# Layers 0 and 1 of a four-layer convolution net: the spectrum, the statistics and the group average spread over the slots of an image

## The reference

```python
# _gn: mean and variance of each pair of channels over an image; (x - mean) / sqrt(var + 1e-5)

def layer0(x, W, b):                       # x is _gn(x)
    offsets = jnp.mean(x, axis=(1, 2)) @ W + b
    dy, dx = jnp.clip(offsets, 0, 28).astype(jnp.int32)   # one pair for an image
    return the image moved down by dy rows and right by dx columns, zeros where nothing comes

def layer1(x, W, b):                       # 3 x 3 convolution of signs
    xq = jnp.where(x >= 0, 1.0, -1.0)
    w_sum = jnp.where(W >= 0, 1.0, -1.0).sum(axis=0)
    return conv(xq, w_sum, padding="SAME") + b.sum(axis=0)

x = x + layer0(_gn(x)); x = x + layer1(_gn(x))
```

## Time and profile before

| what | value |
|---|---|
| median of 3 runs | 4056.27 us (4055.71 to 4059.10) |
| the profiled execution | 4058.18 us |
| its span, first to last instruction | 4056.4 us |
| mean granted TensorE clock | 0.852 of full |
| layers 0 and 1 (last instruction on an `A_` tile) | until 2203 us |

### The profile page before, as it was taken

The page is one execution under the profiler, slowest core; times in us unless marked ns, Lnnn a source line. Parts: engine busy times, 40 slices in busy tenths (PEclk is TensorE's granted clock), DMA queues, the critical chain, the costliest instruction groups (busy, mean ns, idle before and its releaser), DMA issues. The chain is left out here.

```text
span 4056.4 us, 58465 instructions
## 1 busy us (share of the span) xinstructions
PE 3117.6 (77%) x17264; PEld 1421.0 (35%) x17264; DVE 2755.7 (68%) x3864; ACT 1483.0 (37%) x2708; POOL 36.9 (1%) x23
## 2 busy tenths in 40 slices
PE   0277877787877877778786579988998964799997
PEld 0133333333333333233333533333333324344443
DVE  3777665766577656766651557777677744599998
ACT  3455653655455544565433422222222214000000
POOL 0000000000000000000000000000000001000000
PEclk9987886888788877788887589999999976799998
DMA  4666544654466445655433475655665516799998
GB/s 144 176 183 199 160 155 130 203 169 150 131 188 203 141 130 163 203 160 155 139 111 107 93 293 213 251 214 205 240 247 201 219 61 125 270 379 387 390 385 305
DMA packets 272195, 808.65 MB, mean 199 GB/s; under 512 B 85466, under 2 KB 119774, under 8 KB 261108
## 3 DMA queue, kind: packets, MB, share of 16 engines
q1 hardware_dynamic: 212948, 488.15, 37.9%
q10 hardware_dynamic: 58368, 316.72, 20.3%
q0 software_dynamic: 608, 0.63, 0.1%
HBM read 479.39 MB, written 329.56 MB: 199 GB/s over the span
## 5 line engine op out<-in xcount | busy, mean ns | idle before, releaser
L817 DVE SCALAR_TENSOR_TENSOR A_image<-A_cps,A_cbias,A_image 128x896 f32<-128x896 f32 x224 | 257.3, 1149 | 492.0 <-PE A_cps L455 491.7
L1371 ACT ACTIVATE B_junk<-B_im,B_nk 128x896 bf16<-128x896 f32 x224 | 232.8, 1039 | 724.9 <-DVE B_im L1429 585.1
L455 PE MATMUL A_cps<-A_sign,A_cfull 128*128 128x448 bf16 x1344 | 448.9, 421 | 11.3 <-issue 11.3
L595 ACT ACTIVATE A_tout<-A_aps 112x512 f32<-112x512 f32 x448 | 244.5, 589 | 531.9 <-PE A_aps L482 531.5
L482 PE MATMUL A_aps<-a_k_ident,A_image 128*112 128x128 f32 x1792 | 313.5, 331 | 140.5 <-DVE A_image L817 124.5
L1622 PE MATMUL C_ring<-C_im,C_wnorm 128*128 128x448 f32 x896 | 388.9, 573 | 23.0 <-DVE C_ubuf L1679 17.8
L460 PE MATMUL A_cps<-A_sign,A_cedge 32*32 32x448 bf16 x1344 | 405.3, 415 | 0.0
L462 PE MATMUL A_cps<-A_sign,A_cedge 32*32 32x448 bf16 x1344 | 404.9, 414 | 0.0
L1317 PE MATMUL B_ring<-B_im,B_wnorm 128*128 128x448 f32 x896 | 384.5, 570 | 7.7 <-DVE B_wnorm L1400 5.5
L496 PE MATMUL A_vps<-A_tout,a_k_dctj 112*32 112x512 f32 x896 | 289.3, 780 | 118.3 <-ACT A_tout L595 118.2
L1289 PE MATMUL B_ring<-B_rout,iB_k_rowf 128*64 128x512 f32 x896 | 282.2, 714 | 118.3 <-DVE B_rout L1422 118.3
(11 more groups left out here) (193 smaller groups left out, 3436.5 us busy)
## 6 DMA issues: line engine op xcount, KB each, us to landing
A_rin<-in_x SPq DMA_DIRECT2D x2016, 112.0 KB, 2.4
x2s<-A_image ACTq DMA_DIRECT2D x112, 896.0 KB, 4.6
B_im<-x2s SPq DMA_DIRECT2D x112, 896.0 KB, 9.7
x3s<-B_im ACTq DMA_DIRECT2D x112, 896.0 KB
C_im<-x3s SPq DMA_DIRECT2D x112, 896.0 KB, 11.9
out<-C_rout ACTq DMA_DIRECT2D x192, 256.0 KB
out<-C_rout ACTq DMA_DIRECT2D x192, 192.0 KB
out<-C_rout ACTq DMA_DIRECT2D x64, 128.0 KB
```

The lines of the kernel that those rows point to most:

```text
L455: return nc.tensor.matmul(banks[:, s, 0:LPN], cfull[:, tap, :], lines(n, s, slice(0, P), 0, tap), start=(tap == 0), stop=(tap == 2), skip_ ...
```

## The change

- The two tables of tiles start at once and are even: 3 tiles in most slots from slot 0 on. X tiles come first within a slot, in slot 0 ahead of unit 0's add.
- The spectrum's 8 items go two to a slot in slots 0 to 3, one before and one after `forward_cols` and `turn_back`; the rows of an item follow in the next step, the last ones in slot 4. Results go to a bank `wps` of their own, shared with the statistics (`mps` is now its first 16 columns), and to a store buffer `specout` of their own. The copy moves to slot 5 and the store from slot 4 to slot 6.
- The statistics of the next image begin in slots 11 and 12 in place of 13 and 14. Part 2 is cut in two (2 and 4); the second, behind the root, comes after the signs. ACT takes the root in slot 13, and `lower` is in slot 14 ahead of the square.
- The group average is on PE after unit 13's convolution. The signs' semaphore is split in two (`sign_full` for the first piece, `sign_rest`).
- Two squarings of a single column become `tensor_scalar`.

The core of the diff:

```diff
+        specout = sb("specout", [P, BANK])
-        specout = rowspec[:, 0, :]
-        mps = ctx.enter_context(nc.psum_tensor("A_mps", [P, BANK], f32))
+        wps = ctx.enter_context(nc.psum_tensor("A_wps", [P, BANK], f32))
+        mps = wps[:, 0:16]
-        X_BY = [0, 2, 5, 7, 9, 11, 13, 14, 15, 16, 16, 16, 16, 16, 16, 16]
-        S_BY = [0, 0, 0, 1, 2, 3, 4, 6, 8, 10, 13, 16, 16, 16, 16, 16]
+        X_BY = [2, 4, 5, 7, 8, 10, 11, 13, 14, 16, 16, 16, 16, 16, 16, 16]
+        S_BY = [1, 2, 4, 5, 6, 7, 9, 10, 11, 12, 14, 15, 16, 16, 16, 16]
...
             # SP
-                    if has_tail and s == 4:
+                    if has_tail and s == 6:
                         store_spec(b - 1)
...
             # PE
             def statistics(b, i):
-                k = 4 * (b + 1) + i
+                k = average_no(b, i)
+                done = b if i == 4 else b - 1
+                if not isinstance(done, int) or done > 0:
+                    pe.wait_ge(spec_sb, done)
...
             def forward_cols(b, q, p):
-                if p == 0:
-                    if not isinstance(b, int) or b > 0:
-                        pe.wait_ge(spec_sb, b)
-                elif p % 2 == 0:
+                if p % 2 == 0:
...
             def forward_rows(b, k, seq):
                 pe.wait_ge(a_copied, seq + 1)
+                if k == 0:
+                    pe.wait_ge(off_ready, min(b + 3, NB) if isinstance(b, int) else b + 3)
...
-                    last = nc.tensor.matmul(vps[side, P * (k // 2):P * (k // 2 + 1)], con["k_fwdr"][:, g, :], cols[:, g],
+                    last = nc.tensor.matmul(wps[side, P * (k // 2):P * (k // 2 + 1)], con["k_fwdr"][:, g, :], cols[:, g],
...
-            def spectrum(b, k0, base):
-                for k in range(k0, k0 + 4):
+            def spectrum(b, k, base):
+                if k > 0:
+                    forward_rows(b, k - 1, base + ring_t(k - 1))
+                if k < 8:
                     turn_spec(b, k, base + ring_t(k))
-                    if k > k0:
-                        forward_rows(b, k - 1, base + ring_t(k - 1))
-                forward_rows(b, k0 + 3, base + ring_t(k0 + 3))
...
                     if has_v and s < UNITS:
                         conv(b, s)
+                    if has_tail and s < 5:
+                        spectrum(b - 1, 2 * s, ring_base(b))
+                    if has_s and s == 13:
+                        statistics(b, 4)
                     if has_v and s >= 3 and s % 2 == 1:
                         forward_cols(b, q, (s - 3) // 2)
                     if has_v and 1 <= s <= UNITS:
                         turn_back(b, q, s - 1)
-                    if has_tail and s < 2:
-                        spectrum(b - 1, 4 * s, ring_base(b))
-                    if has_s and s == 12:
-                        statistics(b, 4)
-                    if has_x and s >= 13:
-                        statistics(b + 1, s - 12)
+                    if has_tail and s < 4:
+                        spectrum(b - 1, 2 * s + 1, ring_base(b))
+                    if has_x and s in (11, 12, 14):
+                        statistics(b + 1, {11: 1, 12: 2, 14: 3}[s])
...
             # ACT
+                    if has_tail and s < 4:
+                        copy_cols(b - 1, 2 * s, ring_base(b) + ring_t(2 * s))
                     if has_v and 1 <= s <= UNITS:
                         copy_back(b, q, s - 1)
-                    if has_tail and s < 2:
-                        for k in range(4 * s, 4 * s + 4):
-                            copy_cols(b - 1, k, ring_base(b) + ring_t(k))
-                    if has_tail and s == 2:
+                    if has_tail and s < 4:
+                        copy_cols(b - 1, 2 * s + 1, ring_base(b) + ring_t(2 * s + 1))
+                    if has_tail and s == 5:
                         copy_spec(b - 1)
+                    if has_x and s == 13:
+                        root(b + 1)
                     if has_v and s >= 2 and s % 2 == 0:
                         store(b, q, (s - 2) // 2)
+                    if has_x and s == 14:
+                        lower(b + 1, (q + 2) % 3)
                     if has_v and 1 <= s <= UNITS:
                         square(b, q, s - 1)
...
-                    if has_x and s == 14:
-                        root(b + 1)
-                    if has_x and s == 15:
-                        lower(b + 1, (q + 2) % 3)
...
             # DVE
-                    if has_v and s < UNITS:
+                    if has_v and 0 < s < UNITS:
                         add_conv(b, q, s)
                     if has_tail and s == 3:
                         image_statistics(b - 1, far)
-                    if has_v and s in (1, 4, 7):
-                        signs(q, (s + 2) // 3)
+                    if has_x and s in (11, 12):
+                        statistics(b + 1, s - 11, far)
                     for k in x_tiles(s) if has_x else ():
...
                         turn_x(far, k, x_at(k) % RING, tile_loaded(b, x_at(k)))
+                    if has_v and s == 0:
+                        add_conv(b, q, s)
+                    if has_v and s in (1, 4, 7):
+                        signs(q, (s + 2) // 3)
                     for k in s_tiles(s) if has_s else ():
                         add_shifted(b, nxt, k, s_at(k, has_x))
                     if has_s and s == 12:
                         center(b)
                     if has_s and s == 13:
+                        if has_v:
+                            dve.wait_ge(sign_rest, 3 * (b + 1))
                         centered(b, nxt)
-                        if has_v:
-                            dve.wait_ge(conv_full, UNITS * (b + 1))
+                    if has_x and s == 13:
+                        statistics(b + 1, 2, far)
+                    if has_s and s == 13:
                         signs(nxt, 0)
                     if has_x and s == 13:
-                        statistics(b + 1, 0, far)
+                        statistics(b + 1, 4, far)
                     if has_x and s == 14:
-                        statistics(b + 1, 1, far)
-                    if has_x and s == 15:
-                        statistics(b + 1, 2, far)
                         statistics(b + 1, 3, far)
```

More of the change, by code:

```diff
@@ L478, in turn_back @@
                     seq = ring_base(b) + ring_o(b, n, half)
+                    side = ring_o(b, n, half) % 2
                     ring_item(seq)
@@ L481, in turn_back @@
                         first = (2 * n + l // 2) * LPN + 2 * HR * half
-                        last = nc.tensor.transpose(aps[half][0:HR, l * P:(l + 1) * P],
+                        last = nc.tensor.transpose(aps[side][0:HR, l * P:(l + 1) * P],
                                                    image[q][:, first:first + 2 * HR].rearrange("p (j s) -> p s j", s=2)[:, l % 2, :], con["k_ident"][:])
@@ L554, in _ @@
             body(NB - 1, (NB - 1) % 3, True, False, False, True)
-            for s in range(2):
-                spectrum(NB - 1, 4 * s, ring_base(NB - 1) + 36 - 2 * s)
+            for k in range(8):
+                turn_spec(NB - 1, k, ring_base(NB - 1) + 36 + k)
+                if k > 0:
+                    forward_rows(NB - 1, k - 1, ring_base(NB - 1) + 36 + k - 1)
+            forward_rows(NB - 1, 7, ring_base(NB - 1) + 36 + 7)
         @block.scalar
@@ L594, in copy_back @@
                         act.wait_ge(tout_read, PAIRS * b + n // 2)
-                    nc.scalar.activation(tout[n % OUTS][:, half, :], aps[half][0:HR, :], ACT.Copy).then_inc(a_copied, 1)
+                    nc.scalar.activation(tout[n % OUTS][:, half, :], aps[ring_o(b, n, half) % 2][0:HR, :], ACT.Copy).then_inc(a_copied, 1)
             def store(b, q, g):
@@ L618, in copy_spec @@
                 act.wait_ge(spec_full, b + 1)
-                nc.scalar.activation(specout, vps[:, :], ACT.Copy).then_inc(spec_sb, 1)
+                if not isinstance(b, int) or b > 0:
+                    act.wait_ge(spec_stored, 8 * 16 * b)
+                nc.scalar.activation(specout[:], wps[:, :], ACT.Copy).then_inc(spec_sb, 1)
             def square(b, q, n):
@@ L735, in statistics @@
                     link(nc.vector.tensor_scalar(sm[:, 28:29], sm[:, 26:27], 1.0 / NPIX, nx[:], ALU.mult, ALU.add))
-                    link(nc.vector.tensor_tensor(sm[:, 29:30], sm[:, 28:29], sm[:, 28:29], ALU.mult))
+                    link(nc.vector.tensor_scalar(sm[:, 29:30], sm[:, 28:29], sm[:, 28:29], None, ALU.mult))
                     link(nc.vector.scalar_tensor_tensor(out=mv[:, 1:2], in0=sm[:, 27:28], scalar=1.0 / NPIX, in1=sm[:, 29:30],
@@ L854, in image_statistics @@
                 link(nc.vector.tensor_scalar(sm[:, 23:24], sm[:, 22:23], nk[q][:], None, ALU.add))
-                link(nc.vector.tensor_tensor(sm[:, 24:25], sm[:, 23:24], sm[:, 23:24], ALU.mult))
+                link(nc.vector.tensor_scalar(sm[:, 24:25], sm[:, 23:24], sm[:, 23:24], None, ALU.mult))
```

33 lines of the change are left out of this document (21 added, 12 removed).

## The result

| what | before | after |
|---|---|---|
| median of 4 runs each, us | 4055.99 (4053.52 to 4059.10) | 3761.56 (3744.49 to 3783.59) |
| the profiled execution, us | 4058.18 | 3783.59 |
| its span, us | 4056.4 | 3781.8 |
| mean granted TensorE clock | 0.852 | 0.874 |
| layers 0 and 1, until | 2203.1 | 1906.8 |

The ratio is 0.9277, with a 95% interval from 0.9225 to 0.9329: 7.2% faster, 294 us. The forecast was 3760, 7.3% faster, in a range from 3635 to 3890.

The account below looks back on a forecast made before the run. No engine is full; VectorE idles 40.4 us of a 127.1 us steady image, 25.3 for convolutions. Steady images -273, prologue +4, first -10, fifteenth -13, last -4: -296 from 4058, less 2, gives 3760 us, range 3635 to 3890.

Parts of the forecast that it names:

- thirteen steady images: Images with a spectrum in layers 0 and 1: 109.9 us each against 130.9, 21.0 less, times 13 = 273 us.
- fifteenth: The image without x tiles, set by TensorE: 93 us where 106.4 stood, -13, counting five spectrum slots of 7.9 us.
- last image and its spectrum: End of layers 0 and 1: 4 us less, given without a working.
- the waits at units 1, 2 and 13: VectorE's waits for convolutions, 9.94, 9.11 and 5.68 us an image, were taken as removed.
- The load term: VectorE's waits for loads, spectrum stores standing ahead of slot 7's tiles on SyncE: 6.4 us where 9.0 stood.
- The turn: From one image to the next, x tile 0 waits for unit 13's store and square until T0 + 11.5: 3.3 us new idle.
- small waits: VectorE's waits between steps of the statistics, for TensorE's average or ScalarE's root: 6.1 us an image, kept in the sum.
- The averages: Statistics 0 and 1 in slots 11 and 12 delay convolutions 12 and 13, and the adds behind them: 2.4 us.
- between 0 and 14 I take 5 us, weighted by those counts: TensorE's low clock in the spectrum slots: 5 us a steady image, weighted by how many earlier images were long.
- the low stretch in every image: Rival: low clock in about two spectrum slots of each image, 14 us instead of 5, 3877 us; chance 0.17.
- the last sentence of the prediction: Wrong if slots 0 to 4 run mostly at clock 0.5, or spectrum copies stand behind ScalarE's x-tile sums and squares.
- The high clock: Rival: TensorE's clock stays high, clock costs 0 and loads 2 us, 100.5 us an image, 3641 us; chance 0.20.

Follow-up runs that it names:

- run 9: The changed kernel itself once more, unaltered, beside the combinations on the same chip: 3768.15 us, ratio 0.9302.
- runs 1: The changed kernel with the spectrum's items four to a slot in slots 0 and 1 again, as before: 3852.93 us, ratio 0.9472.
- run 4: The changed kernel with the group average again ahead of unit 13's convolution on TensorE, as before: 3863.95 us, ratio 0.9497.
- run 7: The changed kernel with the spectrum's store in slot 11 instead of slot 6: 3685.76 us, ratio 0.9082.
- run 10: The changed kernel with the edits of run 5 and run 7 together: 3612.03 us, ratio 0.8910.
- run 3: The changed kernel with the first two averages of the statistics behind convolutions 12 and 13 on TensorE: 3760.38 us, ratio 0.9258.
- run 6: The changed kernel with the loop of four rounds over three images written out on all engines: 3732.43 us, ratio 0.9175.
- Runs 2: The changed kernel with ScalarE's next spectrum copy moved ahead of the last x tile in slots 1 and 2: 3708.25 us, ratio 0.9114.
- run 5: The changed kernel with ScalarE's last x tile of slots 0 to 2 behind both copies of the next slot: 3691.50 us, ratio 0.9076.
- run 11: The kernel of run 10 with the loops over the steady images written out as well: 3606.22 us, ratio 0.8881.

## Why the prediction was right, and where its terms were off

**The total.** Layers 0 and 1 end 296.3 us earlier, by the same count that was forecast, 296. That is partly chance. The terms are off in both directions, and in the profile of run 9, the same kernel, layers 0 and 1 end at 1892.2, 311 us earlier than before. The terms:

| term | forecast | measured |
|---|---|---|
| prologue, T0 of the first image | +4 | +1.3 |
| first image | -10 | -13.8 |
| thirteen steady images | -273 | -243.4 |
| fifteenth | -13 | -24.8 |
| last image and its spectrum | -4 | -15.6 |

The whole profiled execution fell by 274.6, not 296, since it lost time outside the change. The stretch of 899.2 us from the end of layers 0 and 1 on, first in this execution, then in the one of the same kernel in run 9:

```profile
1906.80:2806.00 899.20, 732.40 (x4078) 325.57 (x4082) 590.66 (x671) 239.09 (x390) 15.80 (x6) 0.86 0.57 211
```

```profile
1892.20:2791.40 899.20, 730.88 (x4168) 328.90 (x4169) 600.26 (x687) 245.53 (x400) 15.80 (x6) 0.89 0.59 219
```

The clock was 0.86 instead of 0.89 there. From the end of layers 0 and 1 to the end the two took 1875.0 and 1854.4 us, before 1853.3. So 3783.59, the highest of the four, carries some 21 us that are not the change's.

**What went.** Right: the waits at units 1, 2 and 13 are gone, and runs 1 and 4 bring them back, the first two and the third, each alone. The load term was right in size and cause, 6.3 for 6.4 us, and run 7 shows the cause: the spectrum's eight stores stand ahead of slot 7's tiles in SyncE's queue. The prediction had 3.4 us for that queue and put another 3 on the engines that loads and stores share. "DMA: Bandwidth & Descriptors", "Issuing engines are not separate DMA queues", of the Trainium skill says that loads and stores run on the same 16 engines whoever issues them. Moved to slot 11, the same stores left a third of the load waits, 24.5 of 78.0 us. What cost was mainly the place in the queue.

**The turn.** X tile 0 came at T0 + 9.6, forecast 11.5; its wait was 2.48 us for 3.3 forecast, and the small waits beside it 3.8 (what is left of 110.7 - 86.3 when the others are taken off) for 6.1. ScalarE's list at the turn, from the first copy at T0 + 1.6 to the last square at T0 + 9.3, took 7.8 us without a pause, where the prediction's items add up to 8.9: the store's issue ran beside the square, and each instruction began a little before the one ahead of it had ended.

**The averages.** 2.4 us were forecast, 4.4 measured in image 6 and 3.4 in the mean of the thirteen. The excess is the clock: the convolution at unit 12 ran in a stretch at 0.58, and in run 10, with the clock high, the two waits are 1.9 us an image. A wait that was there and could be removed bought nothing that could be measured: in run 3 these waits fell by 25.1 us over the thirteen images, and 10.9 of them came back at units 3 and 4.

**The clock: near in size, wrong in cause.** The step "between 0 and 14 I take 5 us, weighted by those counts" took the lengths of before for a chance of the clock. For the three images of 138 to 141 us, 42 of the 62 us in that sum, it was none: they are those behind a jump of the loop. In the changed kernel the same three are 7 to 9 us longer than the others, 1.9 us in the mean of the thirteen, and run 6 brings them back into line. The ordinary images have a low stretch in slots 2 and 3 nearly every time, so the rival "the low stretch in every image" came true in what it saw, but for these images not in its cause, the idling for the statistics at the turn. Only in images 2, 4 and 10 does a long low stretch, of 23.9 us, begin near the turn, at T0 + 5 to 11. Its price was 7.4 us at units 3 and 4, not 14, since it covers one and a half slots. It comes where the last sentence of the prediction named a way to be wrong: TensorE's in-order queue meets ScalarE's x tiles. That was seen and not priced. A count of ScalarE's list would have given the stand, though not what the clock did behind it: a square of the convolved image, two sums and two squares of x tiles are 5.5 us between two copies, from 842.85 to 848.37.

Runs 2 and 5 tie the low stretch to this place, since work moved on ScalarE alone shortens it or takes it away. They do not make a rule of the stand's length. In run 10, image 6, TensorE stood as long as in the changed kernel, now for a turned unit ahead of column matmuls, and the clock stayed at 1.00 (the second row is TensorE alone, columns as above):

```profile
811.04 1.91 PE L509 MATMUL A_vps<-A_tout,a_k_dctj 112*32 112x512 f32 x8 [1.92 <-ACT A_tout L614]
```

```profile
811.10:822.00 10.90, 9.19 (x60) 1.00 0.70 225
```

**The high clock.** That rival, 100.5 us an image and 3641 in all (its own terms add up to 3638), is where run 10 arrives, at 100.1 us an image and 3612.03, and with the parts that it named: load waits of 2.0 us an image and next to nothing for the clock at units 3 and 4 (0.7). It took two edits more than the change had. "Perfetto Trace Analysis", "Matmul Optimizations", of the Trainium skill asks for matmuls in batches, since the engine's power follows its utilization. Run 5 agrees in direction, by closing one stand of 1.95 us to 0.78. As a sufficient condition it does not hold here: TensorE was busy for 13.7 us without a break at 0.51, as in the long row of before.

**The last two images.** For the fifteenth five slots of 7.9 us were counted; four carry two items, and at a clock of 1.00 they took 7.2 each. For the last image the prediction gives its -4 without a working. Its adds no longer wait for four items at a time, and its last add comes at T0 + 80.6 instead of 91.4.

**What stays open.** Why a stand has a low stretch behind it in one place and none in another. The low stretches of 20 to 24 us at T0 + 6 to 11, which run 10 still shows in the three images behind a jump and in one other, were not traced to a cause: TensorE has stands of 0.3 to 0.9 us there in every image, and the clock fell in some images and not in others. Nor is it shown why the ordinary images of the written-out loops take 2 us more; five of run 11's have a low stretch of 6.8 us from T0 + 6.6 on, where run 10 has one such image. The move of the statistics to slots 11 and 12, the bank and the store buffer of their own were not taken back in any run, so what they bring by themselves is not known.

## What to carry to other kernels

When work is spread over the slots of an in-order engine, count also the slots of the engine that empties its buffers: a copy that two items of other work stand ahead of cost more here than the stand itself, because the clock fell behind it. Before lengths that vary are taken for chance, look whether they come at the period of the program's loop. A store that nobody waits for belongs in the queue where the loads behind it have slack; here five slots later were worth 2%.

## What the runs showed of the hardware

- TensorE stood in slot 2, amid small float32 matmuls. Behind stands of 1.94 to 2.12 us (the changed kernel, twelve images) a low stretch of 10.2 or 13.7 us began in eleven; behind 0.96 us (run 2, twelve) in eight; behind 0.77 to 0.98 us (run 5, twelve) in none. Eight stands of 1.92 us elsewhere, at T0 + 46 to 48 in run 10, had no low stretch in the 11 us behind them. So the length of a stand does not settle it.
- A jump of the loop cost the image behind it 7 to 9 us. Of these 3.7 stood before the first add, with 1.7 to 3.8 us of "issue" in TensorE's first convolution; the mean clock of these images was 0.80, that of image 6 0.85.
- Eight stores of the spectrum took SyncE 5.54 us. Five slots later in its queue the same stores left 24.5 us of load waits where 78.0 had been.
- Executions of one kernel spread, and the mean clock goes with them: in run 9 it was 0.886 at 3748.39 us and 0.872 at 3795.76. The changed kernel's spread over 39 us in four runs and 47 in six, those of before over 5.6 us in four and 48 in eleven. In the profiled one 21 us fell on code that the change does not touch.
